# Side work of a selective-state-space kernel: projections of 512 columns instead of 256, softplus products four steps apart instead of two

## The reference, cut to what matters

```
xz = h @ in_w;  xs, z = split(xz);  xs = silu(xs)            # 512 + 512 channels
proj = xs @ xproj_w                                          # 512 for dt, 64 for B, 64 for C
dt = softplus(proj[..., :512] + dt_bias)
hst = hst * exp(dt_t[:, :, None] * A) + (dt_t * x_t)[:, :, None] * B_t[:, None, :]   # 512 x 64 states
y_t = einsum('bds,bs->bd', hst, C_t)                         # for each of 256 times
out = ((y + xs * Dskip) * silu(z)) @ out_w
```

## Time and profile before

| what | value |
|---|---|
| median of 3 runs | 5320.44 us (5316.38 to 5328.83) |
| the profiled execution, its own time | 5325.41 us |
| its span | 5323.7 us |
| first scan starts, last one starts | 107.07 us, 4868.5 us |
| busy: PE, DVE, ACT, POOL | 93%, 89%, 64%, 71% |
| mean granted clock of TensorE | 0.986 |

### The profile page before, as it was taken

How to read it: one execution, slowest core, us unless ns; L and a number is a source line. 1 busy time by engine, 2 the same in 40 slices (tenths; PEclk the granted TensorE clock), 3 DMA queues, 4 the chain that set the end, 5 groups by cost and what they waited for, 6 DMA issues and landing times. The chain is left out here.

```text
span 5323.7 us, 130492 instructions
## 1 busy us (share of the span) xinstructions
PE 4933.5 (93%) x44784; PEld 2685.7 (50%) x44784; DVE 4730.8 (89%) x2419; ACT 3391.4 (64%) x11498; POOL 3755.2 (71%) x6613
## 2 busy tenths in 40 slices
PE   6999999999999999999999999999999999876898
PEld 4555555554555555555555555555555555443444
DVE  2999999999999999999999999999999999996443
ACT  4666666666766766666766667666666766663112
POOL 4787878677787878777787878777877877674211
PEclk8999999999999999999999999999999999998899
DMA  3121211112121211112111211112111211113442
GB/s 107 38 65 42 59 47 51 55 39 61 39 64 45 64 39 51 56 38 61 43 60 45 64 40 50 55 40 60 45 58 41 64 40 40 36 28 108 144 155 67
DMA packets 433144, 306.75 MB, mean 58 GB/s; under 512 B 215920, under 2 KB 336240, under 8 KB 432496
## 3 DMA queue, kind: packets, MB, share of 16 engines
q1 hardware_dynamic: 428272, 294.39, 18.4%
q10 hardware_dynamic: 4224, 4.19, 0.2%
HBM read 187.27 MB, written 111.15 MB: 56 GB/s over the span
## 5 line engine op out<-in xcount | busy, mean ns | idle before, releaser
L886 DVE TENSOR_TENSOR_SCAN b_hs<-b_dA,b_u 128x1024 f32<-128x1024 f32 x2048 | 4544.0, 2272 | 228.8 <-ACT b_u L813 198.8
L1049 PE MATMUL b_ex<-b_dd,b_aw 32*128 32x512 f32 x8192 | 2786.4, 643 | 21.6 <-POOL b_dd L534 15.4
L1036 PE MATMUL b_u<-b_ud,b_bw 32*128 32x256 f32 x16384 | 2327.1, 401 | 262.8 <-DVE b_hs L886 243.7
L795 ACT ACTIVATE b_dA<-b_ex 128x496 f32<-128x496 f32 x4096 | 2305.3, 594 | 165.4 <-PE b_ex L1049 129.6
L1036 PEld LDWEIGHTS b_u<-b_ud,b_bw 32*128 32x128 f32 x16384 | 1419.9, 185 | 1119.0 <-issue 573.9
L813 ACT ACTIVATE b_u<-b_hin 128x32 f32<-128x32 f32 x1792 | 371.0, 207 | 1278.5 <-PE b_u L1036 978.2
L1068 PE MATMUL b_y<-b_hs,b_cw 128*32 128x256 f32 x16384 | 1110.7, 387 | 2.3 <-DVE b_hs L886 2.3
L534 POOL TENSOR_TENSOR b_dd<-b_dr,b_mask 128x512 f32<-128x512 f32 x1024 | 1074.3, 1049 | 51.2 <-DVE b_hs L886 39.7
L543 POOL TENSOR_TENSOR b_ud<-b_ur,b_mask 128x512 f32<-128x512 f32 x1024 | 1085.1, 1060 | 0.0
L1049 PEld LDWEIGHTS b_ex<-b_dd,b_aw 32*128 32x128 f32 x8192 | 873.2, 183 | 83.6 <-ACT b_dA L795 55.6
L1068 PEld LDWEIGHTS b_y<-b_hs,b_cw 128*32 128x32 f32 x16384 | 428.0, 108 | 856.0 <-issue 674.6
(11 more groups left out here) (104 smaller groups left out, 2357.9 us busy)
## 6 DMA issues: line engine op xcount, KB each, us to landing
b_u<-scratch_ut SPq DMA_DIRECT2D x256, 128.0 KB, 2.9
scratch_y<-b_ysb SPq DMA_DIRECT2D x128, 256.0 KB, 2.1
scratch_xs<-b_xs SPq DMA_DIRECT2D x64, 256.0 KB, 2.4
scratch_sz<-b_sd SPq DMA_DIRECT2D x64, 256.0 KB, 2.2
scratch_dt<-b_sd SPq DMA_DIRECT2D x64, 256.0 KB, 2.1
scratch_ut<-b_uT SPq DMA_DIRECT2D x64, 256.0 KB, 2.5
b_ur<-scratch_ut SPq DMA_DIRECT2D x1024, 16.0 KB
b_dr<-scratch_dt SPq DMA_DIRECT2D x1024, 16.0 KB, 1.7
```

Of the source, the lines that this page charges most:

```text
L795: nc.scalar.activation(dA[:, j % NDA, h, :, 1:TC], src[:, :, 1:TC], ACT.Exp).then_inc(exp_done, 1)
L886: nc.vector.tensor_tensor_scan(hs[:, v, :, :, kp].rearrange("p d t -> p (d t)"), dA[:, j % NDA, :, :, :].rearrange("p h d t -> p (h d t)") ...
L1036: ins = nc.tensor.matmul(dst[:, :, tb, :], bw[row(r), c % 2, tb, :], ud[row(r), j // 2 % NPR, tb, :, :], start=(tb == 0), stop=(tb == NTB ...
L1049: nc.tensor.matmul(e[bank_of[what]][:, :], aw[row(r), p % DIRS, v, :, :].rearrange("p b s -> p (b s)"), dd[row(r), (p * PAIRS + j // 2) % ...
```

## The change

It makes one product over both sequences (512 columns) where there were two of 256. `project_xz` issues its two matmuls in steps s and s+2, `project_dt` its four in steps s, s+2, s+4, s+6. ACT reads 512 columns at once, Copy in one step and Tanh in the next, Relu in one step and Abs in the next. `plus_one` of block i now stands in step 4i+4, for blocks 5, 6, 7 in steps 90, 102, 108. `take_dt` stands in steps 28+16j and 29+16j, and `log_part` follows: L686 is in step 33+16j. On POOL `times_sigmoid` of blocks 0 to 4 stays at 4i+5, those of 5, 6, 7 stand in 95, 102, 108. The difference stays in step 33+16j; correction, sum and dt·x come 4, 8 and 12 steps later. The last transpose of dt·x moves from step 94 to 96. Side jobs hold their banks longer: 4 steps for xz (was 1 twice), 8 for dt (was 3 twice).

```diff
-        XZ_SLOT = ((0, 2), (4, 6), (8, 10), (12, 14), (16, 18), (86, 88), (98, 100), (104, 106))
-        DT_SLOT, DT_SPAN = (22, 38, 54, 70), 3
-        BC_SLOT, BC_SPAN = (32, 48), 3
-        UT_SLOT, UT_SPAN = (64, 80, 82, 94), (2, 2, 1, 1)
+        XZ_SLOT, XZ_SPAN = (0, 4, 8, 12, 16, 86, 98, 104), 4
+        DT_SLOT, DT_SPAN = (22, 38, 54, 70), 8
+        BC_SLOT, BC_SPAN = (32, 48), 4
+        UT_SLOT, UT_SPAN = (64, 80, 82, 96), (3, 3, 2, 1)
...
@@ POOL: unit
-                    yield from wait_steps(2)
+                    yield from wait_steps(9)
                     for j in range(JB):
-                        yield from wait_steps(3)
-                        if norm_next and j >= 2:
-                            normalise(c, 2 * j - 4)
+                        difference(q, j)
                         yield from wait_steps(2)
                         if norm_next and j == 1:
                             variance(c)
                         elif norm_next and j >= 2:
+                            normalise(c, 2 * j - 4)
+                        yield from wait_steps(2)
+                        correction(q, j)
+                        yield from wait_steps(2)
+                        if norm_next and j >= 2:
                             normalise(c, 2 * j - 3)
                         yield from wait_steps(2)
-                        yield from softplus(q, j)
-                        yield from wait_steps(2)
+                        sum_dt(q, j)
+                        yield from wait_steps(4)
+                        times_x(q, j)
+                        yield from wait_steps(4 if j + 1 < JB else 2)
                     times_sigmoid(q, JB + 1)
-                    yield from wait_steps(12)
+                    yield from wait_steps(7)
@@ ACT: take_xz, take_dt, unit
-                    nc.scalar.activation(dst[:, cols], job_bank(n)[:, 0:SEQ], ACT.Copy, scale=0.5)
+                    nc.scalar.activation(dst, job_bank(n)[:, :], ACT.Copy, scale=0.5)
+                    yield
...
-                    nc.scalar.activation(pre[:, m % 2, cols], job_bank(n)[:, 0:SEQ], ACT.Relu, bias=bias)
-                    nc.scalar.activation(ey[:, cols], job_bank(n)[:, 0:SEQ], ACT.Abs, bias=bias).then_inc(freed, 1)
+                    nc.scalar.activation(pre[:, m % 2, :], job_bank(n)[:, :], ACT.Relu, bias=bias)
+                    yield
+                    if m:
+                        act.wait_ge(nd_made, 2 * m)
+                    nc.scalar.activation(ey[:, :], job_bank(n)[:, :], ACT.Abs, bias=bias).then_inc(freed, 1)
...
                     for i in range(JB + 1):
-                        take_xz(q, i, 0)
+                        if i:
+                            plus_one(q, i - 1)
                         yield from wait_steps(2)
-                        take_xz(q, i, 1)
+                        yield from take_xz(q, i)
                         yield
-                        plus_one(q, i)
-                        yield
+                    plus_one(q, JB)
                     yield from wait_steps(2)
                     for j in range(JB):
-                        yield from wait_steps(2)
-                        take_dt(q, j, 0)
-                        yield from wait_steps(4)
-                        take_dt(q, j, 1)
+                        yield from wait_steps(6)
+                        yield from take_dt(q, j)
@@ PE: project_xz (project_dt likewise, four matmuls)
-                    for k in range(MB):
-                        last = nc.tensor.matmul(job_bank(n)[:, 0:SEQ], win[:, k, i * P:(i + 1) * P],
-                                                hT[:, q % DIRS, k, b * SEQ:(b + 1) * SEQ], start=(k == 0), stop=(k == MB - 1))
+                    for k in range(MB):
+                        if k:
+                            yield from wait_steps(2)
+                        ins = nc.tensor.matmul(job_bank(n)[:, :], win[:, k, i * P:(i + 1) * P], hT[:, q % DIRS, k, :],
+                                               start=(k == 0), stop=(k == MB - 1))
```

More of the change, by code:

```diff
@@ L218, in job_slots @@
             for i in range(SILUS):
-                for b in range(CB):
-                    at[XZ_SLOT[i][b]] = (base + XZ_JOB[i] + b, 1)
+                at[XZ_SLOT[i]] = (base + XZ_JOB[i], XZ_SPAN)
             for j in range(JB):
-                for b in range(CB):
-                    at[DT_SLOT[j] + 4 * b] = (base + DT_JOB[j] + b, DT_SPAN)
+                at[DT_SLOT[j]] = (base + DT_JOB[j], DT_SPAN)
                 at[UT_SLOT[j]] = (base + UT_JOB[j], UT_SPAN[j])
@@ L341, in unit @@
                     if q + 1 < PASSES:
-                        hold(sp, sp_passed, full, base + DT_JOB[JB - 1] + CB)
+                        hold(sp, sp_passed, full, base + DT_JOB[JB - 1] + 1)
                         load_wxp(q + 1)
@@ L472, in times_sigmoid, with difference @@
                     nc.gpsimd.tensor_tensor(dst, dst, th[:, i % 2, :], ALU.mult).then_inc(silu_made, 1)
-                def softplus(q, j):
+                def difference(q, j):
                     m = q * JB + j
@@ L478, in softplus, with correction, sum_dt @@
                     nc.gpsimd.tensor_tensor(ey[:, :], wy[:, :], ey[:, :], ALU.subtract).then_inc(nd_made, 1)
-                    yield from wait_steps(2)
+                def correction(q, j):
+                    m = q * JB + j
                     pool.wait_ge(nd_made, 2 * m + 1)
                     nc.gpsimd.tensor_tensor(ln[:, :], ln[:, :], ey[:, :], ALU.subtract).then_inc(nd_made, 1)
-                    yield from wait_steps(2)
+                def sum_dt(q, j):
+                    m = q * JB + j
                     pool.wait_ge(nd_made, 2 * m + 2)
@@ L488, in softplus, with times_x @@
                     nc.gpsimd.tensor_tensor(sd[:, j, :], pre[:, m % 2, :], ln[:, :], ALU.add).then_inc(dt_made, 1)
[L489 to L490 removed]
+                def times_x(q, j):
+                    pool.wait_ge(dt_made, q * JB + j + 1)
                     if j >= 2:
@@ L759, in unit @@
                         if i == JB + 1:
-                            yield from wait_steps(5)
+                            yield from wait_steps(6)
                             take_ut(q, 3)
+                            yield from wait_steps(2)
+                        elif i == JB + 2:
+                            yield from wait_steps(2)
+                        else:
                             yield from wait_steps(4)
[L763 to L766, removed]
                     if norm_next:
@@ L933, in turn_x, with project_xz @@
                     last.then_inc(full, 1)
-                def project_xz(q, i, b):
-                    n = first_job(q) + XZ_JOB[i] + b
+                def project_xz(q, i):
+                    n = first_job(q) + XZ_JOB[i]
                     bank_free(n)
                     for k in range(MB):
-                        last = nc.tensor.matmul(job_bank(n)[:, 0:SEQ], win[:, k, i * P:(i + 1) * P],
-                                                hT[:, q % DIRS, k, b * SEQ:(b + 1) * SEQ], start=(k == 0), stop=(k == MB - 1))
-                    last.then_inc(full, 1)
@@ L943, in project, with project_dt @@
-                def project(n, cols, b, gap):
+                        if k:
+                            yield from wait_steps(2)
+                        ins = nc.tensor.matmul(job_bank(n)[:, :], win[:, k, i * P:(i + 1) * P], hT[:, q % DIRS, k, :],
+                                               start=(k == 0), stop=(k == MB - 1))
+                    ins.then_inc(full, 1)
+                def project_dt(q, j):
+                    if j == 0:
+                        pe.wait_ge(wxp_loaded, (q + 1) * 16)
+                        pe.wait_ge(silu_made, q * SILUS + JB)
+                    n = first_job(q) + DT_JOB[j]
@@ L945, in project @@
                     bank_free(n)
                     for k in range(JB):
-                        ins = nc.tensor.matmul(job_bank(n)[:, 0:SEQ], wxp[:, k, cols], xs[:, k, b * SEQ:(b + 1) * SEQ],
+                        if k:
+                            yield from wait_steps(2)
+                        ins = nc.tensor.matmul(job_bank(n)[:, :], wxp[:, k, j * P:(j + 1) * P], xs[:, k, :],
                                                start=(k == 0), stop=(k == JB - 1))
-                        if k == 1:
-                            yield from wait_steps(gap)
@@ L951, in project @@
                     ins.then_inc(full, 1)
[L953 to L957, removed]
-                def project_bc(q, b):
-                    yield from project(first_job(q) + BC_JOB[b], slice(DI, PW), b, BC_SPAN - 1)
+                def project_bc(q, b):
+                    n = first_job(q) + BC_JOB[b]
+                    bank_free(n)
+                    for k in range(JB):
+                        if k == JB // 2:
+                            yield from wait_steps(2)
```

(12 more changed lines are left out.)

46 lines of the change are left out of this document (18 added, 28 removed).

## The result

The changed kernel takes **5623.38 us**, the median of 4 runs (5620.47 to 5631.77). The kernel before took 5322.0 on the same chip (5316.38 to 5328.83). The ratio is 1.0568, its 95% interval 1.0550 to 1.0587. The forecast was 5575 us, the range 5445 to 5690. The profiled execution took 5621.98 us with a span of 5620.3; its mean granted clock is 0.955, where it was 0.986.

What follows compares the result with a forecast made beforehand. DVE's scans bound the kernel, delayed by waits on ACT, PE and POOL. +11.0 us a pass times 15 is 165; with -2.5 before the loop and +92 for the clock, +254.5: 5575 us, range 5445 to 5690.

Steps and rivals of the forecast that it cites:

- The difference: POOL's first softplus product waits longer for ACT's L686; scans 34, 50, 66, 82 each 1.86 us later, 7.4 a pass.
- `times_sigmoid` of blocks 6 and 7: POOL's product now shares a step with ACT's `plus_one`; scans 103 and 109 each 2.60 us later, 5.2 a pass.
- Steps 18 to 33: `times_sigmoid` of blocks 3 and 4 adds 0.8 us a pass; one wide Abs at step 28's table load saves 0.1.
- What the change takes away: Savings at scans 91 and 87, the sum's wait and crowding, less a later transpose: -2.4 us a pass.
- (3): POOL's sum L488 no longer waits for a transfer at step 37: -0.9 us a pass with the product's crowding.
- (4): POOL's products no longer crowd at steps 51 to 55 and the like: -0.15 us a pass.
- PE and the banks: Wide products 0 to -2.4 us a pass, longer bank holds 0 to +4; both taken as 0.
- The clock: Six stalls a pass idle PE; three of four lower TensorE's clock at 1.6 us: 108 us, +92 net.
- the forecast's rival: Every stall causes a long clock fall of 2.94 us: 265 us instead of 108, 5732 us; chance 0.10.
- The clock did not stay up: Rival: the stalls do not lower TensorE's clock, 5467 us; chance 0.16.
- The banks added 1.5 us a pass and not 4: Rival: even steps also pay for PE's longer bank holds, +4 us a pass, 5635 us; chance 0.09.
- The faster rival: POOL's difference waits no longer than 3.1 us and spacing by four only relieves it: about 5267 us; chance 0.05.

Runs made afterwards that it cites:

- e5: Changed kernel with only POOL's difference one step later (34+16j instead of 33+16j); 5412.61 us, ratio 1.0169.
- e6: Changed kernel with ACT's Relu and Abs of take_dt back in one step, so minus one (L692) comes a step earlier; POOL untouched; 5435.72 us, ratio 1.0204.
- e2: Changed kernel with POOL's four softplus products and every `times_sigmoid` two steps later; 5249.26 us, ratio 0.9879.
- e4: Kernel before the change with only POOL's new order (softplus products four steps apart, block 5's `times_sigmoid` in step 95); 5270.56 us, ratio 0.9918.
- e7: e4 (narrow products) with all of POOL's softplus products and `times_sigmoid` two steps later, last transpose at step 96; 5233.16 us, ratio 0.9825.
- e3: Changed kernel with two PE side jobs (`turn_b`, third `turn_inputs`) and their ACT reads two steps later; 5633.56 us, ratio 1.0596.
- e1: Changed kernel with only POOL's four softplus products of each dt block two steps later; 5399.75 us, ratio 1.0162.
- e8: e7 with ACT's reads of block 5 in steps 88 and 89, away from step 86's table load, bank held longer; 5237.23 us, ratio 0.9836.

## Why the prediction was right, and where it was not

**The difference: right.** Predicted was 1.86 us at each of four scans, 7.4 a pass. Measured were 1.90, 1.80, 1.68 and 1.67, together 7.05. e5 and e6 show the cause from both sides: the distance in steps between L692 and L475.

**`times_sigmoid` of blocks 6 and 7: right.** Predicted 5.2, measured 2.59 and 2.50, 5.1. e2 takes it away. Steps 18 to 33: predicted +0.8 - 0.1, measured +0.76.

**What the change takes away: about right in sum, not in its parts.** Scan 91 gained 0.86, as predicted, scan 87 gained 0.67 for 0.55, but scans 88 to 90 lost 0.42. Behind scan 34 the clock's loss hides the gain of the sum's vanished wait. e4 shows that wait and the crowding together: scans 35 to 40 went from 2.12 to 0.68, more than the 1.05 of my (3) and (4); some of it are falls of the clock that no longer come.

**PE and the banks: I took 0, and it was not 0.** Scans 1 to 17 lost 0.49 us a pass. Scans 67 to 71 and 83 to 86 are 0.74 and 0.49 later in e2 than in e7, though neither stalls there. In e2 `turn_b` and `turn_inputs` (L977, L986) still wait some 1.4 us each for a bank in front of just these scans, and e7 has no such wait; that they are the reason was not tested by itself:

```profile
PEld b_ex L986 <- ACT b_dA L799: 21.0, 15, 1.7
PEld b_ex L977 <- ACT b_dA L799: 20.8, 15, 1.4
```

e2 against e7 puts the whole at 1.5 us a pass, inside the 0 to +4 that the text allowed. Its sign of being wrong, a move of the distance in steps 56 to 62 by more than 0.1 us, did not come: the mean is 0.02 us shorter than before.

**The clock: the mis-sized term.** "I take three of four to lower the clock, at 1.6 us (mostly the short kind)": of the 90 stalls 69 were followed by a fall, 0.77 of them. The share was right, with some luck: the same six stalls gave 80 falls in e3. The size was not. Scan 50 gives the measure, for there the stall is the same 2.4 us in all passes, but the clock fell in only 4 of 15. The granted clock around scan 50 in the fourth, the third and the ninth pass (window, its length, PE busy with count, clock, DMA share, GB/s), two windows each:

```profile
1189.00:1194.00 5.00, 3.99 (x35) 1.00 0.27 69
1194.00:1199.00 5.00, 5.00 (x47) 1.00 0.06 13
```

```profile
868.00:873.00 5.00, 3.93 (x28) 0.88 0.21 64
873.00:878.00 5.00, 5.00 (x44) 0.78 0.12 27
```

```profile
2778.00:2783.00 5.00, 3.92 (x20) 0.68 0.21 60
2783.00:2788.00 5.00, 5.00 (x40) 0.63 0.11 26
```

And DVE in the third and the ninth pass, beside the fourth's above:

```profile
869.38 4.46 DVE L889 TENSOR_TENSOR_SCAN b_hs<-b_dA,b_u 128x1024 f32<-128x1024 f32 x2 [2.60 <-ACT b_u L816]
875.65 13.38 DVE L889 TENSOR_TENSOR_SCAN b_hs<-b_dA,b_u 128x1024 f32<-128x1024 f32 x6 [1.81 <-ACT b_u L816]
```

```profile
2778.92 4.46 DVE L889 TENSOR_TENSOR_SCAN b_hs<-b_dA,b_u 128x1024 f32<-128x1024 f32 x2 [2.38 <-ACT b_u L816]
2786.39 13.38 DVE L889 TENSOR_TENSOR_SCAN b_hs<-b_dA,b_u 128x1024 f32<-128x1024 f32 x6 [3.01 <-ACT b_u L816]
```

The two scans behind the stall and the way to the third take 4.72 us at full clock (1193.98 - 1189.26), 6.27 with a short stretch at the 1.2 GHz level, and 7.47 with one twice as long. So in these passes a short fall costs 1.55, a long one 2.75; over all passes the means are 1.4 and 2.4. Of the 69 falls 46 were long (6.8 us in the records of the granted clock) and 23 short (3.4 us). Set against passes without a fall (behind scans 50 and 103 in this kernel, behind the others in e1 and e2), the scans from each of the six stalls to the next lose 142 us in the 15 passes to falls, 2.1 each, where I had 6 x 0.75 x 1.6 x 15 = 108. I took the short kind from six falls behind stalls of 0.86 us; the new stalls are 2.3 to 3.2 us, and behind such a stall the first pass had shown the long kind once. Both kinds occur, the long one twice as often, and the mean of 2.1 lies between my 1.6 and the 2.94 of that one case. The 2.94 alone would have been no better: 6 x 0.75 x 2.94 x 15 is 198, 56 too much where 108 is 34 too little. 142 instead of 108 is 34 us of the 48 that the forecast fell short. For the rest PE's share is the likely place; that is argued from the table, not shown.

One premise of the term was wrong too. It took PE to be idle for 1.7 us or more at each of the six stalls. At scans 34 and 50 PE has a single idle piece of 1.07 us. Here they are in the fourth pass:

```profile
1149.38 1.67 PE L1053 MATMUL b_ex<-b_dd,b_aw 32*128 32x512 f32 x4 [1.07 <-ACT b_dA L798]
...
1189.75 1.67 PE L1053 MATMUL b_ex<-b_dd,b_aw 32*128 32x512 f32 x4 [1.07 <-ACT b_dA L798]
```

The first was followed by a fall in 15 passes of 15, the second in 4.

The Trainium skill, TensorE: Matmul & The Clock Gate, section "HAM oscillation — how this bites in real kernels", has a kernel whose clock goes down at each of its waits. By that rule there would be 90 falls. The trace agrees behind scans 34, 66, 82 and 109, 15 times each, and not behind scan 50 (4 times) and scan 103 (5 times), where the stalls are as long. The waits in the page's example are 3 to 5 us, longer than nearly all of these stalls, so it says less about them than the forecast's rival took from it.

**The rivals.** The clock did not stay up. Not all falls were long. The difference's wait did grow. The banks added 1.5 us a pass and not 4. The faster rival's figure, 5267 for spacing alone without a longer wait, is nearly what e4 measured (5270.56), though there the chain was left as it was.

**What stays open.** What decides whether a stall lowers the clock. Its length does not: a stall of 2.4 us at scan 50 lets the clock stand 11 times of 15 and one of 2.3 at scan 66 never. The longest idle piece of PE does not either: it is 1.07 us at scans 34 and 50, with 15 and 4 falls here and 10 and 12 in e3, where both stalls are the same. Which part of the 1.5 us a pass is the width of the products and which the hold of the banks; no kernel here parts them.

## What to carry to other kernels

Count steps between the instruction that raises a semaphore and the one that waits for it, on each edge between two in-order queues, before and after an edit. An edit that moves a producer by one step and leaves its consumer costs the whole carried chain behind that consumer, here 1.8 us each time, and moving the consumer by one step gives it all back. Where a stall leaves TensorE idle, add a price for the clock; here it came to 142 us beside the 182 of the stalls themselves (7.05 + 5.1 us in 15 passes). The length of a stall did not tell here whether the clock would fall, so keep a range for this term. And test the parts of such a change apart: the new order on POOL alone was worth 45 us, with late products 90, and the wide products cost some of it.

## What the runs showed of the hardware that was not expected

- How much a short idle time of TensorE can cost: in the changed kernel 392.5 us of the loop ran at the 1.2 GHz level, in 69 stretches; in e2 there were 2, in e4 1. A single idle piece of 1.07 us in front of scan 34 was followed by a fall in every pass.
- The number of falls at one place is not a property of that place: with the same stalls at scans 50 and 103 the changed kernel had 4 and 5 falls in 15 passes, e3 12 and 13.
- Two waits of PE of up to 3.9 us, 15 times each, cost next to nothing beside a stall of the whole chain: with them moved away (e3) the scans behind them gained 0.4 us a pass, and the kernel was not faster.
- Taking ACT's work away from beside a table load saved nothing when it was paid for with a longer hold of a bank: in e8 the 0.56 us gained at scan 87 came back as 1.17 behind it.
